# Moving the row products of a recurrence from GpSimd to VectorE, and taking the reciprocals two group pairs later

## The reference, cut to what matters

```python
x = layernorm(x0)                        # (2, 4096, 2048)
xx = prev - x                            # difference to the previous token
xk, xv, xr, xg = x + xx * tm_k, x + xx * tm_v, x + xx * tm_r, x + xx * tm_g
r, k, v = xr @ Wr.T, xk @ Wk.T, xv @ Wv.T
g = sigmoid(xg @ Wg.T)
w = exp(-exp(time_decay)); eu = exp(time_first)
# scan over the tokens, ek = exp(k_t), a = b = 0 at the start:
#   out = (a + eu * ek * v_t) / (b + eu * ek)
#   a, b = w * a + ek * v_t, w * b + ek
attn = sigmoid(r) * wkv                  # wkv: the outputs of the scan
o = layernorm((attn * g) @ Wo.T)
y = x0 + o * silu(ffn(x))                # ffn: ternary weights from weight_f
```

## Time and profile before

| | |
|---|---|
| time before, median of 2 runs | 1506.35 us (1490.6 and 1522.1) |
| the profiled execution, its own time | 1474.11 us |
| its span on the slowest core (core 7) | 1472.5 us |
| spans of the 8 cores | 1460.0 to 1472.5 us |
| core 2 | 1472.4 us |
| TensorE (matmul) busy on core 7 | 824.9 us (56%) |
| ScalarE busy | 494.0 us (34%) |
| VectorE busy | 513.7 us (35%) |
| GpSimd busy | 156.5 us (11%) |

### The profile page before, as it was taken

How to read it: one execution, slowest core, us unless ns; L and a number is a source line. 1 busy time by engine, 2 the same in 40 slices (tenths; PEclk the granted TensorE clock), 3 DMA queues, 4 the chain that set the end, 5 groups by cost and what they waited for, 6 DMA issues and landing times. The chain is left out here.

```text
span 1472.5 us, 11824 instructions; the slowest of 8 cores (1460.0 to 1472.5 us)
## 1 busy us (share of the span) xinstructions
PE 824.9 (56%) x3834; PEld 362.0 (25%) x3834; DVE 513.7 (35%) x469; ACT 494.0 (34%) x660; POOL 156.5 (11%) x228
## 2 busy tenths in 40 slices
PE   2532220057947579999911767260297879884200
PEld 0110000023524245544400323020143334331000
DVE  0059999200000004764015044555710000000597
ACT  4632222112221121122212347546253433428221
POOL 0002222000000000011122022222200000000011
PEclk8555555579979799999965988685598999999555
DMA  3438788673352733653155442433534444400387
GB/s 115 144 91 273 252 276 251 192 248 126 123 162 71 244 115 101 187 174 122 40 186 138 108 125 80 121 97 98 181 93 122 121 128 126 127 20 0 96 252 223
DMA packets 79069, 211.64 MB, mean 144 GB/s; under 512 B 11424, under 2 KB 11424, under 8 KB 79008
## 3 DMA queue, kind: packets, MB, share of 16 engines
q1 hardware_dynamic: 54432, 139.57, 33.4%
q0 software_dynamic: 15360, 53.49, 9.8%
q10 hardware_dynamic: 9216, 17.83, 3.6%
HBM read 166.81 MB, written 39.85 MB: 140 GB/s over the span
## 5 line engine op out<-in xcount | busy, mean ns | idle before, releaser
L983 PE MATMUL rgo_ps<-mov_rg,rgo_wbf 128*128 128x512 bf16 x1024 | 238.9, 398 | 209.1 <-DMA mov_rg<-sxg 71.9
L405 PE MATMUL g1ps<-mov_kv,g1wbf 128*128 128x512 bf16 (+1 forms) x1536 | 261.0, 335 | 101.7 <-DMA mov_kv<-sxk 41.6
L822 ACT ACTIVATE rgo_wbf<-rgo_mw 128x512 bf16<-128x512 f32 x192 | 120.0, 633 | 273.9 <-DMA rgo_mw<-wr 99.7
L405 PEld LDWEIGHTS g1ps<-mov_kv,g1wbf 128*128 128x128 bf16 x1536 | 132.9, 101 | 229.7 <-issue 114.3
L983 PEld LDWEIGHTS rgo_ps<-mov_rg,rgo_wbf 128*128 128x128 bf16 x1024 | 103.6, 102 | 344.5 <-issue 235.2
L983 PE MATMUL rgo_ps<-wkv_sb,rgo_wbf 128*128 128x512 bf16 x512 | 115.5, 389 | 18.6 <-ACT sr_sb L959 10.3
L405 PE MATMUL g1ps<-xn_sb,g1wbf 128*128 128x512 bf16 x512 | 110.8, 379 | 1.1 <-ACT g1g2s L340 1.1
L269 DVE CAST g1wbf<-g1mwstg 128x1024 bf16<-128x1024 f32 x24 | 16.7, 694 | 239.2 <-PE g1ps L405 103.9
L333 ACT ACTIVATE g1row<-g1ps 128x512 f16<-128x512 f32 (+1 forms) x96 | 44.5, 492 | 146.3 <-PE g1ps L405 136.4
L573 PE MATMUL ps_sc<-fs_a,ones 128*1 128x512 f16 x64 | 32.3, 608 | 88.4 <-ACT fs_a L618 88.4
L881 DVE TENSOR_TENSOR_SCAN zar<-w_sb,r_vvr 128x1152 f32<-128x1152 f32 x16 | 41.6, 2597 | 106.2 <-POOL r_vvr L854 106.0
(11 more groups left out here) (114 smaller groups left out, 883.2 us busy)
## 6 DMA issues: line engine op xcount, KB each, us to landing
g1mwstg<-wf SPq DMA_DIRECT2D x64, 512.0 KB, 4.7
g1mwstg<-wk SPq DMA_DIRECT2D x32, 512.0 KB, 5.9
g1mwstg<-wv SPq DMA_DIRECT2D x32, 512.0 KB, 4.8
rgo_mw<-wr SPq DMA_DIRECT2D x64, 256.0 KB, 3.7
rgo_mw<-wg SPq DMA_DIRECT2D x64, 256.0 KB, 3.3
rgo_mw<-wo SPq DMA_DIRECT2D x64, 256.0 KB, 3.2
xstg<-x SPq DMA_DIRECT2D x16, 576.5 KB, 4.5
xst<-x SPq DMA_DIRECT2D x16, 512.0 KB, 5.3
```

The lines of the kernel that those rows point to most:

```text
L405: mm = e.matmul(bank[:, :t1 - t0], wbf[hh % 2][:, ic, oc * 128:(oc + 1) * 128], s["mov"][:, ic, t0:t1], start=(ic == 0), stop=(ic == CH - 1))
L822: e.activation(wbf[ss % 2][:, ic, :], mwstg[jj % 2][:, :], AF.Copy).then_inc(sem["scs"], 1)
L983: mm = e.matmul(bank[:, :t1 - t0], wbf[ss % 2][:, ic, oc * 128:(oc + 1) * 128], phs[p]["mov"][:, ic, t0:t1], start=(ic == 0), stop=(ic == ...
```

## The change

The diff does four things. GpSimd loses its two products and keeps the loads. VectorE makes them at the head of each chain: it waits for the row's loads (`st0`/`st1`), scales the first 128 tokens of `ekr` with `cs_sb` as a scalar operand, and multiplies `vvr` by `ekr`. The tile `cs_tile`, its two preparing instructions and the semaphore between the engines go. `RP` becomes 8 + 2 ci (its two upper limits, 38 and 63, are not passed: row 15 stands at 38), so that rows 0 to 3 are in slab r1, 4 to 7 in r2, 8 to 11 in r3, and 12 to 15 at groups 32 to 38. And the loads of rows 2 and 3 wait for chains 0 and 1.

```diff
--- before.py
+++ after.py
@@ -57,7 +57,7 @@
 
     sem = {n: e0(nc.semaphore(n)) for n in
            ("sl", "sw0", "sw1", "scv", "scs", "smm", "sev", "st0", "st1",
-            "sv", "ss", "sden", "srd", "sgp", "sg1")}
+            "sv", "ss", "sden", "srd", "sg0", "sg1")}
     cnt = {n: 0 for n in sem}
 
     def snap():
@@ -743,7 +743,6 @@
                for i in range(NROW)]
         zar = ec(nc.sbuf_tensor("zar", [128, 1 + T_ALL], F32))
         zbr = ec(nc.sbuf_tensor("zbr", [128, 1 + T_ALL], F32))
-        cs_tile = ec(nc.sbuf_tensor("cs_tile", [128, LANE], F32))
         ps = [ec(nc.psum_tensor("rgo_ps%d" % i, [128, 512], F32))
               for i in range(8)]
         blk = es.enter_context(nc.Block())
@@ -794,7 +793,8 @@
                 i += 1
                 svord[(kind, l)] = i
         NSV = i
-        RP = {ci: min(4 + 2 * ci, NRG - 1) for ci in range(CH)}
+        RP = {ci: min(8 + 2 * ci, NR + NSG - 2, NRG - 1)
+              for ci in range(CH)}
 
         swtot = [b["sw0"], b["sw1"]]
         swtarget = [0] * (NSS * CH)
@@ -842,40 +842,32 @@
 
         @blk.gpsimd
         def _(e):
-            for ci in range(CH + 2):
-                if ci >= 2:
-                    cj = ci - 2
-                    m = cj % NROW
-                    e.wait_ge(sem["st%d" % (cj % 2)], st_row[cj])
-                    e.wait_ge(sem["ss"], b["ss"] + 1)
-                    e.tensor_tensor(ekr[m][:, 0:LANE], ekr[m][:, 0:LANE],
-                                    cs_tile[:, :], OP.mult)
-                    e.drain()
-                    inc(e.tensor_tensor(vvr[m][:, :], ekr[m][:, :],
-                                        vvr[m][:, :], OP.mult), "sgp")
-                if ci < CH:
-                    if ci >= NROW:
-                        e.wait_ge(sem["sv"],
-                                  b["sv"] + svord[("q", ci - NROW)])
-                    stp = "st%d" % (ci % 2)
-                    e.dma_start(ekr[ci % NROW][:, :],
-                                sek[ci, :, :]).then_inc(sem[stp], 16)
-                    e.dma_start(vvr[ci % NROW][:, :],
-                                svd[ci, :, :]).then_inc(sem[stp], 16)
+            for ci in range(CH):
+                if ci >= NROW:
+                    e.wait_ge(sem["sv"], b["sv"] + svord[("q", ci - NROW)])
+                elif ci >= 2:
+                    e.wait_ge(sem["sden"], b["sden"] + ci - 1)
+                stp = "st%d" % (ci % 2)
+                e.dma_start(ekr[ci % NROW][:, :],
+                            sek[ci, :, :]).then_inc(sem[stp], 16)
+                e.dma_start(vvr[ci % NROW][:, :],
+                            svd[ci, :, :]).then_inc(sem[stp], 16)
 
         @blk.vector
         def _(e):
             e.memset(zar[:, 0:1], 0.0)
             e.memset(zbr[:, 0:1], 0.0)
-            e.memset(cs_tile[:, :], 1.0)
-            e.drain()
-            inc(e.tensor_scalar(cs_tile[:, :], cs_tile[:, :],
-                                cs_sb[:, 0:1], None, OP.mult), "ss")
             e.drain()
             for kind, l in v_events:
                 if kind == "chain":
                     m = l % NROW
-                    e.wait_ge(sem["sgp"], b["sgp"] + l + 1)
+                    e.wait_ge(sem["st%d" % (l % 2)], st_row[l])
+                    e.drain()
+                    e.tensor_scalar(ekr[m][:, 0:LANE], ekr[m][:, 0:LANE],
+                                    cs_sb[:, 0:1], None, OP.mult)
+                    e.drain()
+                    e.tensor_tensor(vvr[m][:, :], ekr[m][:, :],
+                                    vvr[m][:, :], OP.mult)
                     e.drain()
                     wbc = w_sb[:, l:l + 1].broadcast_to([128, T_ALL])
                     e.tensor_tensor_scan(zar[:, 1:], wbc, vvr[m][:, :],
```

## The result

| | before | after |
|---|---|---|
| median of all timed runs | 1496.72 us (10 runs) | 1470.35 us (11 runs) |
| ratio | | 0.9825, 95% interval 0.9766 to 0.9883 |
| profiled execution, its own time | 1474.11 us | 1449.49 us |
| span of the slowest core | 1472.5 us (core 7) | 1448.0 us (core 3) |
| GpSimd busy, of that core | 156.5 us | 105.7 us |

What follows compares the result with a forecast made beforehand. ScalarE's serial cast blocks and rounds bound the kernel; moved reciprocals cancel, leaving waits removed: 19.85 us on core 7, 18.2 on core 2, which ends last. The 18.3 us gain, rounded to 19, gives 1506.35 - 19 = 1487 us, range 1456 to 1508.

Steps and rivals of the forecast that it cites:

- What bounds the stage: In r, g and o: TensorE waits for ScalarE's unbroken alternation of cast blocks and rounds, with 19.85 us waiting for chains.
- Part 1, the products: On VectorE: scaling 0.29 us, product 0.78, chain 8.8, row's step 10.3 in place of 16; low end chosen.
- The slack: Each slab's fourth chain ends at 13.8 us from its first round, its reciprocal due at 17.7: slack 3.9 us.
- That needs both parts of the change.: No wait for chains needs moved products and later reciprocals, which leave three finished rows in front of every slab.
- Part 2, the landing: VectorE waits for row loads instead, landing in 4.4 us, 11.1 at worst; cost nothing.
- Part 3, the walk along ScalarE: Two reciprocals move later: ScalarE ahead 9.7, 11.2, 20.7, 29.6 us through r, then 19.6 after giving back 10.0 in g1.
- One of my own signs of being wrong: In the changed profile, a cast block outside 31 to 34 us would show the prediction wrong.
- Rounding up for the lighter block of r2: In the total: the 18.3 us gain was rounded up to 19 for r2's lighter cast block.
- Casts faster as a whole: Rival: blocks r2, r3, g0, g1 fall to 29.1 us, 14.3 us more gain, 1473 us; chance 0.08.
- Nothing given back in g: Rival: the reciprocals added at groups 36 and 38 lie under matmuls, 29.6 us stay, 1477 us; chance 0.08.
- The waits stay: Rival: ScalarE waits in four slabs again, needing a chain over 12.7 us; 1506 us if gain wholly eaten; chance 0.09.
- Blocks crowded by the row loads: Rival: row loads slow cast blocks, deciding from 5 us more each; at 37.8 us blocks, 1507.5 us; chance 0.04.

Runs made afterwards that it cites:

- e4: The changed kernel with the first scan of each chain run four times; 1498.8 us in its one execution.
- e6: The changed kernel with four staging tiles for the weights in place of two; median 1347.8 us, ratio 0.9084 to the kernel before.
- e5: The changed kernel with the reciprocals of two rows at one group, so 16 table loads fall away; median 1453.1 us, ratio 0.9749 to the kernel before.
- e1: The changed kernel with the reciprocals put back to group 4 + 2 ci, so only the products move; median 1459.8 us, ratio 0.9869 to the kernel before.
- e3: The changed kernel with the first scan of each chain run twice; 1458.8 us in its one execution.

## Why the prediction was right, point by point

**What bounds the stage.** Right: ScalarE's serial order of cast blocks and rounds. e4 put 47.4 us of waits into it and got 48.5 back, e6 took 149 us of blocks out (384.7 to 235.9) for 106 of stage, until TensorE took over. e5 took 14.7 us of rounds out for 8.2 of stage, since its blocks grew by 6.4.

**Part 1, the products.** Right, and at the low end as chosen: 0.25 and 0.76 us against 0.29 and 0.78, a chain of 8.7 us (931.84 to 940.57), a row's step of 10.4 against 10.3.

**The slack.** Right: 3.9 forecast, 3.7 in the timeline and by e4.

**"That needs both parts of the change."** Wrong. I argued that chains 0 to 2 of a slab are done because the lead leaves three finished rows in front of it. It does, but the row order gives it anyway: with the old places the slabs begin with rows 2, 6 and 10 in place of 0, 4 and 8, and again the first three chains do not depend on a reciprocal of this slab; only the fourth stands behind the first q. e1 has no wait. The number didn't hang on this step.

**Part 2, the landing.** Right: in the new profile the scaling waits for a landing once, 10.4 us in the opening, where VectorE had stood 15.3 us before the first scan. The row buffers landed in 4.5 us (median) against 4.4 before, 10.7 at the worst against 11.1. The delay of GpSimd's loads that the Trainium skill's rule (SBUF — State Buffer, "SBUF: two separate sides") allows was at most the 0.25 us of the scaling, and no run shows it.

**Part 3, the walk along ScalarE.** By means over the cores, between the blocks: 9.9 ahead at r2 (9.7 forecast), 11.5 behind r1's rounds (11.2), 21.1 behind r2's (20.7), 30.2 behind r3's (29.6), and 20.4 behind g1's (19.6). The stretches between blocks sum to 123.4 before and 103.0 after, 20.4 us; forecast were 19.6. The blocks changed by 1.2 us in sum: the opening's two fell by 1.5, r2's became lighter by 1.3 as expected, r3's rose by 0.5, g0's fell by 0.7 and g1's rose by 2.0. One of my own signs of being wrong did fire: on core 3 g1's block took 37.0 us (1011.68 to 1048.70) and r2's 30.8, both outside 31 to 34. That bound came from core 7 alone; over the 8 cores g1's block took 33.4 to 37.4 us before the change as well.

**The total.** 1487 was forecast, 1470.35 measured, inside the range. Part of the gap isn't the change: the median of before moved from 1506.35 in two runs to 1496.72 in ten. The gain was 26.4 us where 19 were forecast. One term was too small, the wait: I took core 2, with 18.2 us of it, as the core that ends last. The mean wait is 20.0 us, and with 1.2 us of shorter blocks the stage shrank by 21.3, on the two cores that had ended last by 16.8 (core 2) and 23.5 (core 7). The profiled executions lie further apart, 24.8 us in the mean of the cores' spans, and 3.3 of these are ahead of the stage: its first load came at 749.8 us before and at 746.5 after, in work that the change doesn't touch (means of the cores, from the start of the span). That part is luck of the executions, and what is left up to 26.4 is within the interval, which begins at 17.5. Rounding up for the lighter block of r2 was a guess of size, not a reading. And the range, 1456 to 1508, took in every rival, so a time inside it says little: what bears out the mechanism are the waits, the starts of the blocks, e1 and e4. The forecast within 2% is neither borne out nor refuted, since the interval of the ratio, 0.9766 to 0.9883, lies on both sides of that line.

**The rivals.** Casts faster as a whole: no, 1.2 us in 385. Nothing given back in g: no, the wait before g2 rose by 9.5 us. The waits stay: not at this chain length; e4 shows them at 16.6 us of chain, and the threshold of 12.7 lies between e3 (11.4) and e4. Blocks crowded by the row loads: not by the 5 us each that it needed; g1's grew by 2.0.

## What to carry to other kernels

When an engine that sets the pace waits for a chain through two others, measure the chain's slack against the pacing engine's round, slab by slab; while there is slack the chain's speed is worth nothing (e3), and once the chain is late each microsecond of lateness counts fully (e4). Such a gain is no fixed number: it was 21 us of the stage beside 30 us blocks and 49 beside 18 us ones. And before moving work between engines, look at the pacing engine's own idle time: here a block waited 20 us for loads through two staging tiles, and taking 12 of them away with four tiles was worth five times the whole change.

## What I had not expected of the hardware

In the kernel before, GpSimd stood 1.7 to 5.2 us between its two instructions of a row (3.30 us), mostly with "issue" as the releaser. Between them the program has a drain (`e.drain()`), so that the product reads what the scaling wrote, and right in front of the scaling GpSimd had issued the two loads of another row. The timeline of core 7 shows two such loads, and behind the second the one row that had none in front of it (start 1047.11):

```profile
908.14 0.55 POOL L863 DMA_DIRECT2D r_vvr<-svd  x1
...
1038.62 0.55 POOL L863 DMA_DIRECT2D r_vvr<-svd  x1
1039.19 0.44 POOL L851 TENSOR_TENSOR r_ekr<-r_ekr,cs_tile 128x128 f16<-128x128 f16 x1
1044.79 2.36 POOL L854 TENSOR_TENSOR r_vvr<-r_ekr,r_vvr 128x1152 f16<-128x1152 f16 x1 [5.16 <-DMA r_vvr<-svd]
1047.11 0.43 POOL L851 TENSOR_TENSOR r_ekr<-r_ekr,cs_tile 128x128 f16<-128x128 f16 x1
1047.69 4.41 POOL L854 TENSOR_TENSOR r_vvr<-r_ekr,r_vvr 128x1152 f16<-128x1152 f16 x1 [0.15 <-issue]
```

The view of DMA issues (windows 908 to 909 and 1038.5 to 1039) gives the time from issue to landing of the two loads, in us at the end of the line:

```profile
r_vvr<-svd POOLq DMA_DIRECT2D x1, 288.0 KB, 4.1
r_vvr<-svd POOLq DMA_DIRECT2D x1, 288.0 KB, 6.0
```
